# Memory attention on one core: softplus of the decay rates moved behind the gradient's squares, key scores and first layer in one product per batch, SiLU by ScalarE

## What is computed

```python
k, v, q = (causal_conv4(h @ W.T) for W in (Wk, Wv, Wq))           # [B, S, 64]
alpha = mean(sigmoid(h @ aW.T + ab) * 0.1)
eta   = mean(sigmoid(h @ eW.T + eb) * 0.9 + 0.05)
theta = mean(softplus(h @ tW.T + tb) * 0.1)
for each chunk of 128 tokens:                                      # 8 chunks
    g = grad over W of |silu(k @ W1.T) @ W2.T - v|^2, at the chunk's first state, * 0.1
    g = g * min(1 / |g|, 1)
    for t in chunk: S = eta*S - theta*g[t];  W = (1 - alpha)*W + S; keep W[t]
    out[t] = silu(q[t] @ W1[t].T) @ W2[t].T
out = rmsnorm(out @ Wo.T) * norm_g * (h @ gW.T + gb)
```

## Time and profile before

| what | value |
| --- | --- |
| median of 3 runs | 854.41 us (850.83 to 855.55) |
| profiled execution, its own time | 863.48 us |
| its span | 861.6 us |
| mean granted TensorE clock | 0.901 of full speed |
| TensorE busy | 721.4 us (84%) |
| VectorE busy | 605.4 us (70%) |
| ScalarE busy | 436.1 us (51%) |
| GpSimd busy | 249.9 us (29%) |

### The profile page before, as it was taken

One profiled execution on the slowest core, in us unless ns is written; L12 is line 12 of the kernel. 1 busy time (PEld: TensorE's weight loads), 2 busy tenths in 40 slices (PEclk: granted clock), 3 DMA queues, 4 the chain that ended last, 5 costly groups with the idle time before them and its releaser, 6 DMA issues. The chain is left out here.

```text
span 861.6 us, 15519 instructions
## 1 busy us (share of the span) xinstructions
PE 721.4 (84%) x5689; PEld 632.9 (73%) x5689; DVE 605.4 (70%) x1311; ACT 436.1 (51%) x1034; POOL 249.9 (29%) x185
## 2 busy tenths in 40 slices
PE   4449799995767999999999999999878238899996
PEld 2238799994566878888788887878756127799996
DVE  1877577843485978798888987977763655787761
ACT  1525457540636565665866568565432504475550
POOL 0053511314221143250623506142232045413202
PEclk9769899997888989999898999999977659999999
DMA  9975624613101012040130303103030723616300
GB/s 335 409 276 168 251 63 164 194 24 129 49 0 50 2 49 99 2 147 2 51 99 22 125 2 99 51 1 99 1 97 2 244 78 111 207 52 226 115 13 31
DMA packets 57858, 89.19 MB, mean 104 GB/s; under 512 B 6592, under 2 KB 48704, under 8 KB 57664
## 3 DMA queue, kind: packets, MB, share of 16 engines
q1 hardware_dynamic: 45808, 70.18, 23.5%
q0 software_dynamic: 3840, 10.49, 3.6%
q10 hardware_dynamic: 8144, 7.61, 3.0%
HBM read 74.63 MB, written 22.02 MB: 112 GB/s over the span
## 5 line engine op out<-in xcount | busy, mean ns | idle before, releaser
L626 PE MATMUL ps<-moe_normedT_high,weights_high_up 128*128 128x320 f32 x256 | 85.3, 333 | 11.4 <-DVE moe_hidden_low L484 7.2
L484 DVE SCALAR_TENSOR_TENSOR moe_hidden_low<-ps,moe_hidden_high 128x256 fp32r<-128x256 f32 x128 | 54.0, 422 | 40.7 <-ACT moe_hidden_high L589 36.5
L628 PE MATMUL ps<-moe_normedT_high,weights_low_up 128*128 128x320 f32 x256 | 82.4, 322 | 0.0
L627 PE MATMUL ps<-moe_normedT_low,weights_high_up 128*128 128x320 f32 x256 | 82.4, 322 | 0.0
L626 PE MATMUL ps<-weights_high_down,moe_hidden_high 128*128 128x256 f32 x256 | 73.4, 287 | 0.8 <-issue 0.8
L1079 POOL TENSOR_TENSOR att_o_rs<-att_o_mean,minus_half 128x4 f32<-128x4 f32 x16 | 16.2, 1013 | 197.3 <-DVE att_o_mean L1323 197.3
L628 PE MATMUL ps<-weights_high_down,moe_hidden_low 128*128 128x256 f32 x256 | 71.5, 279 | 0.8 <-issue 0.8
L627 PE MATMUL ps<-weights_low_down,moe_hidden_high 128*128 128x256 f32 x256 | 71.4, 279 | 0.0
L626 PEld LDWEIGHTS ps<-moe_normedT_high,weights_high_up 128*128 128x128 f32 x256 | 51.2, 200 | 14.2 <-DVE moe_hidden_low L484 6.1
L567 ACT CAST weights_high_down<-weights_raw_down 128x256 fp32r<-128x256 f32 x96 | 35.0, 408 | 42.2 <-PE ps L628 27.7
L588 ACT ACTIVATE moe_shared<-ps 128x64 f32<-128x64 f32 x128 | 29.0, 227 | 51.3 <-PE ps L628 44.7
(11 more groups left out here) (292 smaller groups left out, 2159.0 us busy)
## 6 DMA issues: line engine op xcount, KB each, us to landing
weights_raw_up<-in_w SPq DMA_DIRECT2D x16, 1024.0 KB
weights_raw_down<-in_w SPq DMA_DIRECT2D x16, 1024.0 KB
first_xt<-in_xT SPq DMA_DIRECT2D x8, 1024.0 KB, 7.9
weights_rows<-x SPq DMA_DIRECT2D x8, 1024.0 KB, 5.6
out_x<-weights_rows SPq DMA_DIRECT2D x8, 1024.0 KB, 4.4
weights_rows<-x ACTq DMA_DIRECT2D x7, 1024.0 KB, 5.5
weights_rows<-x SPq DMA_DIRECT2D x2, 512.0 KB, 4.4
weights_raw_up<-in_w_x SPq DMA_DIRECT2D x1, 704.0 KB
```

Of the source, the lines that this page charges most:

```text
L484: v.scalar_tensor_tensor(hidden_low[i][:, f, :], ps[:, 2 + (KF * i + f) % 3, WHOLE[i]], 0.0, hidden_high[i][:, f, :].bitcast(F32), ALU.max ...
L626: mm(dst, high_l, high_r, start=start, stop=False)
L627: mm(dst, high_l, low_r, start=False, stop=False)
L628: return mm(dst, low_l, high_r, start=False, stop=stop)
```

## The change

- Key scores and the first layer become one product per batch: the queries and W1 lie side by side in a tile QW (128 + 64 columns), and `queries_hidden` multiplies each batch's keys by 192 columns. Its first four batches go to pair A, the last four to pair C.
- SiLU is one ScalarE function (Silu) and, for its slope, a Tanh of half the argument: slope = 0.5 * (1 + hid - (hid - 1) * tanh). The sigmoids of alpha and eta are Tanh as well, with the scales folded into the rates. VectorE's two multiplications by the sigmoid are gone.
- `thetas` (Abs, Exp, Ln) of chunk c moves from the end of ScalarE's step c-1 to step c, between the squares of the gradient and the copy of the key/value projection; a Silu on one column follows it. Chunk 0's stays in the prologue.
- `turn_x` fills BB first and then A, and waits for the key squares and for P1; VectorE's key norms come after the first half of the gated output.
- The state is kept once less (2 x 64 columns instead of 3 x 64).

```diff
@@ VectorE
-            def scores(c):
-                dve.wait_ge(qk_made, c + 1)
-                v.tensor_tensor(P1[:], wide(A), M[:], ALU.mult).then_inc(p1_ready, 1)
-
-            def hidden(c, first):
-                dve.wait_ge(sig_ready, c + 1)
-                if not first:
-                    dve.wait_ge(hid_m_ready, c)
-                v.tensor_tensor(hid[:], wide(C)[:, :, 0:D], sig_h[:], ALU.mult).then_inc(hid_ready, 1)
+            def scores(c):
+                for h, src in enumerate((A, C)):
+                    dve.wait_ge(bend_ready if h else half_bent, c + h)
+                    last = v.tensor_tensor(in_fours(P1, h), key_products(src)[:, :, :, 0:CH], in_fours(M, h), ALU.mult)
+                last.then_inc(p1_ready, 1)
...
-            def second_hidden(c, par):
-                dve.wait_ge(sig2_ready, c + 1)
-                v.tensor_tensor(hid2[:], wide(DD), sig_h2[:], ALU.mult).then_inc(hid2_ready, 1)
...
                 if not last:
                     scores(c + 1)
+                gated_output(c, par, 0)
+                if not last:
                     key_norms(c + 1, 1 - par)
-                    hidden(c + 1, False)
-                gated_output(c, par, 0)
@@ ScalarE, last line of thetas
+                s.activation(unread[:], t["minus_half"][:, 0:1], ACT.Silu)
...
-            def hidden(c, first):
-                act.wait_ge(pre_made, c + 1)
-                if not first:
+            def hidden(c, h):
+                act.wait_ge(qk_made, 2 * c + h + 1)
+                if h == 0:
                     act.wait_ge(slope_ready, c)
-                s.activation(sig_h[:], wide(C)[:, :, 0:D], ACT.Sigmoid).then_inc(sig_ready, 1)
+                    act.wait_ge(hid_m_ready, c)
+                src = key_products(C if h else A)[:, :, :, CH:]
+                last = s.activation(in_fours(hid, h), src, ACT.Silu)
+                if h:
+                    last.then_inc(hid_ready, 1)
+                s.activation(in_fours(bend, h), src, ACT.Tanh, scale=0.5).then_inc(bend_ready if h else half_bent, 1)
...
-                s.activation(sig_h2[:], wide(DD), ACT.Sigmoid).then_inc(sig2_ready, 1)
+                s.activation(hid2[:], wide(DD), ACT.Silu).then_inc(hid2_ready, 1)
...
                 gradients(c)
+                if not first:
+                    thetas(c, par, False)
                 if not last:
                     kv_projection(c + 1)
...
                 if not last:
-                    thetas(c + 1, 1 - par, False)
+                    hidden(c + 1, 0)
                     keys(c + 1, False, final)
-                    hidden(c + 1, False)
+                    hidden(c + 1, 1)
@@ TensorE
-                for h, dst in enumerate((A, BB)):
+                for h, dst in enumerate((A, BB) if first else (BB, A)):
                     pe.wait_ge(x_normed, B * c + HALF * (h + 1))
                     if not first:
-                        pe.wait_ge(p1_ready if h == 0 else knorm_ready, c)
+                        pe.wait_ge(p1_ready if h else k_squared, c)
...
+            def queries_hidden(c, par):
+                pe.wait_ge(q_conv, TAPS * c + TAPS)
+                pe.wait_ge(state_copied, 2 * c)
+                pe.wait_ge(gate_read, 4 * c + 4)
+                for h, dst in enumerate((A, C)):
+                    if h:
+                        pe.wait_ge(gram_copied, c + 1)
+                        pe.wait_ge(lg_read, c)
+                    for j in range(HALF):
+                        b = h * HALF + j
+                        last = mm(key_products(dst)[:, j // 2, j % 2, :], KV[par][0:D, b, :], QW[0:D, b, :],
+                                  start=True, stop=True)
+                    last.then_inc(qk_made, 1)
...
                 keys(c + 1, 1 - par)
-                queries(c + 1, 1 - par)
-                hidden(c + 1, 1 - par, False)
+                queries_hidden(c + 1, 1 - par)
```

More of the change, by code:

```diff
@@ L860, in __init__ @@
         self.x2T = x2T.rearrange("p (k n) -> p k n", k=KH)
-        self.state = start[:, 0:3 * D * B].rearrange("p (b n) -> p b n", b=B)
+        self.state = start[:, 0:2 * D * B].rearrange("p (b n) -> p b n", b=B)
         self.norm_g = start[:, 3 * D * B:3 * D * B + H]
@@ L940, in memory_attention @@
     THETA, KNORM = two("THETA", [P, B]), two("KNORM", [P, B])
-    state, read_w = [given.state, sb("state1", [P, B, 3 * D])], given.read_w
-    sig_h, hid, slope = sb("sig_h", [P, B, D]), sb("hid", [P, B, D]), sb("slope", [P, B, D])
+    state, read_w = [given.state, sb("state1", [P, B, 2 * D])], given.read_w
+    bend, hid, slope = sb("bend", [P, B, D]), sb("hid", [P, B, D]), sb("slope", [P, B, D])
     hid_m = sb("hid_m", [P, B, 2, D])
@@ L1419, in turned @@
                     act.wait_ge(gate_made, 4 * c)
-                for h, src in enumerate((A, BB)):
+                for h, src in enumerate((A, BB) if first else (BB, A)):
                     act.wait_ge(x_turned, 2 * c + h + 1)
@@ L1471, in sigmoids @@
                     act.wait_ge(ends_ready, c)
-                s.activation(sig_ae, (BB if first else A).rearrange("p a n -> p (a n)"), ACT.Sigmoid,
-                             bias=b_ae[:, 0:1]).then_inc(ae_sig, 1)
+                s.activation(sig_ae, (BB if first else A).rearrange("p a n -> p (a n)"), ACT.Tanh,
+                             bias=half_b_ae[:, 0:1], scale=0.5).then_inc(ae_sig, 1)
             def rates(c, first):
@@ L1534, in new_state @@
                 new = wide(C)
-                s.copy(state[1 - par][:, :, 0:D], new[:, :, 0:D])
-                s.copy(state[1 - par][:, :, D:3 * D], new).then_inc(state_copied, 1)
+                s.copy(QW[0:D, :, CH:], new[0:D, :, 0:D])
+                s.copy(state[1 - par][:], new).then_inc(state_copied, 1)
                 s.copy(read_w[0:D, :, 0:D], new[0:D, :, D:P]).then_inc(state_copied, 1)
@@ L1613, in _ @@
             thetas(0, 0, True)
-            hidden(0, True)
+            first_hidden()
             step(0, 0, True, False)
@@ L1727, in hidden, with hidden_turned @@
                 last.then_inc(pre_made, 1)
-            def hidden_turned(c):
+            def hidden_turned(c, first=False):
                 pe.wait_ge(consts, 16 * len(loads))
                 pe.wait_ge(hid_ready, c + 1)
+                pe.wait_ge(bend_ready, c + 1)
+                if not first:
+                    pe.wait_ge(p1_ready, c + 1)
                 for b in range(B):
@@ L1750, in second_hidden @@
                     for rows in (slice(0, D), slice(D, P)):
-                        mm(wide(DD)[rows, b, :], state[par][:, b, rows], QAB[:, b, :], start=True, stop=False)
+                        mm(wide(DD)[rows, b, :], state[par][:, b, 0:D], QAB[:, b, :], start=True, stop=False)
                     for rows in (slice(0, D), slice(D, P)):
@@ L1766, in retrieve @@
                     for rows, b in pair_of(s):
-                        mm(paired[rows, s, :], state[par][:, b, 2 * D:3 * D], hid2_ab[:, b, :], start=True, stop=False)
+                        mm(paired[rows, s, :], state[par][:, b, D:2 * D], hid2_ab[:, b, :], start=True, stop=False)
                     for rows, b in pair_of(s):
@@ L1918, in _ @@
             queries(0, 0)
-            hidden(0, 0, True)
+            hidden(0)
             step(0, 0, True, False)
```

73 lines of the change are left out of this document (43 added, 30 removed).

## The result

The change makes the kernel slightly slower: 860.34 us median of 9 runs (854.72 to 865.14) against 854.41 (850.83 to 857.70, 9 runs), ratio 1.0063 with a 95% interval of 1.0032 to 1.0094. By the ratio that is +5.4 us, between +2.7 and +8.0. Slower was forecast, but with +12.5 us more than twice as much; 860.3 lies inside the stated range of 852 to 877.

What follows compares the result with a forecast made beforehand. TensorE's order was taken to bound the steps. Tails -24.5 and +2.2, heads +24.6 and -2.4, clock +12 and +2, last tail -1.4 gave +12.5 us: 867 us, own range 860 to 876, with rival 1 852 to 877.

Steps and rivals of the forecast that it cites:

- the stall: Head: TensorE's second turn waits 3.3 us for the result's first-half copy, starting 13.7 us after the hidden layer's turning (U).
- The block: Moved softplus plus one-column Silu on ScalarE, between gradient squares and key/value copy: 5.9 us, with three table loads.
- The clock: TensorE drops to half clock behind each head's wait: 2.0 us per head, bounds 0 and 3.4, +12 in all.
- The six heads: From the hidden layer's turning to the new state, chunks 1 to 6: +24.6, less 2.4, plus 12 for the clock.
- Rival 1: Same stall in the heads, but the clock holds: -1.5 us, 853 us, no change; chance 0.18.
- The tails: Seven step ends, new state to the hidden layer's turning: -24.5, +2.2 and +2 for loop jumps, -1.4 for the last.
- Two times: +2.2: Two tails where TensorE's loop jumps back: the old stall, no longer hidden, starts the hidden layer's turning 1.1 us later.
- I take it low, +1 each: Two tails with the loop's jump: TensorE's clock assumed low, +1 us each, +2 in all.
- 3.5 us less per tail: Each of seven tails, at full clock: the hidden layer's turning ends at 469.0 instead of 472.55, -24.5 us in all.
- that is not what decides the tail: Tail: merged products save TensorE 1.0 to 1.9 us, but this saving was said not to decide the tail.
- 3 (Silu and Tanh with different tables): Silu and Tanh need different tables, three more loads per tail: +27 us, 894 us or more; chance 0.05.
- 2: Exp and Ln share a table, one load fewer: block 4.6 us, stall 2.0, worth 7.7 us; 845 if clock holds; chance 0.13.

Runs made afterwards that it cites:

- experiment 3: Changed kernel with one table for Exp and Ln, it and the Silu/Tanh table loaded in ScalarE waits, none in the softplus block; ratio 0.9719 to before.
- experiment 4: Changed kernel with Exp and Ln replaced by Square, so no softplus and no loads in its block; ratio 0.9714 to before.
- experiment 2: The filler: changed kernel with 22 unread TensorE products in the wait for the copy of the result's first half, steps 1 to 6; ratio 0.9966 to before.
- experiment 5: Changed kernel with Exp and Ln from one table loaded at the block's head, two loads in the block instead of three; ratio 0.9908 to before.
- experiment 6: Changed kernel with key scores and first layer as two products per batch (128 and 64 columns) again; ratio 1.0126 to before.
- experiment 7: Changed kernel with the two products per batch apart and the eight batches' gram products as one, using batch 0's weights; ratio 1.0174 to before.
- experiment 1: Changed kernel with the next chunk's softplus put back at the end of ScalarE's step, before the new Silu and Tanh; ratio 1.0128 to before.
- experiment 8: Changed kernel with the softplus back at the step's end, its one Exp/Ln table loaded in ScalarE's wait for the outputs' first half; ratio 0.9907 to before.
- experiment 9: Kernel before with Exp and Ln replaced by Square, so no softplus and no table switches; ratio 0.9784 to before.
- experiment 10: Kernel before, computing everything, with one Exp/Ln table loaded in ScalarE's wait for the outputs' first half; ratio 0.9830 to before.

## Why the prediction was right in kind and wrong in size

**What bounds the kernel, and the stall: right.** The block came out at 5.93 us (5.9 forecast), the squares' end at U + 5.9 (U + 5.8), the second turn at U + 13.7 (U + 13.7), its wait at 3.0 us (3.3). Experiments 3 and 4 show the cause: with the loads out of the block the wait is gone. Three loads in a row behind the squares, the wait for L1581 in six steps, half clock behind it: all as listed under what the changed profile would show.

**The clock: right in this trace, a little dear.** I took 2.0 us per head. The filler gives 1.8, the two kinds of heads of experiment 5 give 1.6. The six heads together were forecast at +34.2 us (24.6 - 2.4 + 12) and measured at +32.2. Rival 1, the clock that holds, did not occur in the profiled execution of the changed kernel. It did behind the same wait of 3 us in six of the twelve heads of experiments 6 and 7, and at 1.9 us in four heads of six. That all six heads of the changed kernel paid for the clock is thus no property of the wait's length, and the other eight executions, which have no trace, may have paid less or more.

**The tails: this step failed, by size.** Forecast -21.7 us (-24.5, +2.2, +2, -1.4), measured -28.4. Two terms were mis-sized:
- *"Two times: +2.2" and "I take it low, +1 each".* I carried the stall of the earlier trace rows into the new tail, 4.2 us in all. It does not occur there: all five tails of steps 1 to 5 take 34.0 us, and the branch back takes 0.2 us instead of 3.3 and 3.5. Experiment 6 shows that each stall would have cost 3.9 us (38.8 against 34.9), more than I thought; two of them would have added 7.8 us, by estimate, and brought the sum near the forecast. It isn't the merging that removes it, since the slow branch is there with merged products in experiments 1, 2 and 8. Why it is gone in the changed kernel stays open.
- *"3.5 us less per tail".* Measured are 3.9 (37.9 to 34.0 in most plain tails), some 0.4 more. ScalarE's second Tanh was over at 462.72, 3.56 us after the products began, against 3.8 in my schedule. The products took 2.86 us, not 2.6, and "that is not what decides the tail" was wrong as well: in experiment 6 the 0.9 us that TensorE needs more appears in every plain tail.

The two tails with the jump gained 8.4 us where the forecast has 2.8; the other five make up the rest of the 6.7 us between forecast and measured tails. The remainder is the heads' 2.0, in the same direction.

**Why that spoiled the sum.** The forecast was the difference of two terms of 34 and 22 us; the true ones are 32.2 and 28.4. They are off by 6% and by 24%, and the difference of +12.5 becomes +3.8, with 5.4 (2.7 to 8.0) measured. That the range held the time is partly luck. It had no bound for a tail that gains more: its own part, 860 to 876, varied the clock and slow plain tails only, and 860.3 lies at its edge for another reason than the cheap clock that this edge stands for. Only rival 1 took it down to 852.

**The rivals.** 3 (Silu and Tanh with different tables) is refuted: 23 loads in the attention part instead of 24, none between Silu and Tanh. 2 did not occur in the changed kernel, but its mechanism is real when it is asked for: with one table for Exp and Ln the wait is 1.1 us shorter (experiment 5). The Trainium skill counts 2.66 us for a switch ("ScalarE: Activation LUTs", What ACT_TABLE_LOAD costs). The traces disagree, also in the new order: from the start of a load to that of the next activation in the block it is 1.29 to 1.30 us. The set with both Exp and Ln that the Trainium skill names (same page, Table sets) serves both functions in experiment 3.

## What to carry to other kernels

A table load waits for no data: in experiment 3 two loads a step lay in waits of ScalarE and cost nothing. So it belongs into one of that engine's waits, with a table that serves all functions of the block; moving the block with its loads from one critical chain to another only moves the cost. Before moving work on an in-order engine, count what is queued behind it at the new place against the slack there: here 5.9 us met 1.6. A stall of TensorE can have a second price behind it, half clock over dense work, which came in some heads and not in others of the same code. And where a forecast is the difference of two large terms, its range should come from theirs.

## What the runs showed of the hardware

- An idle TensorE of 1.9 us was followed by 3.4 us at half clock in two heads and by full clock in four, with the same instructions (experiment 5); one of 3 us was followed by it in all six heads of the changed kernel and in three of six in experiments 6 and 7 each. With 2.7 us of products that nobody reads in the wait (experiment 2) it did not occur in any of the six.
- Where TensorE's loop of two steps jumps back, the branch takes 3.3 to 4.3 us in some kernels (before, experiments 2, 6, 7, 8, 9, 10, and one jump of two in experiment 1) and 0.2 us in others (changed, experiments 3, 4, 5, and the other jump of experiment 1). TensorE starts nothing for 1.6 to 2.6 us at a slow branch, or for 1.2 to 1.3 in experiment 2, unless it waits for ScalarE there anyway (experiments 1 and 8).
- The slow branches go together with packets on the queue that fetches instructions. From 395 to 605 us, where both jumps of each kernel lie, that queue brings 17 or 18 packets in the kernels with two slow branches, 10 in experiment 1, and 0 or 1 in those with none; in the kernel before, packets start at 413.3 and 516.7 us, within the branches of 412.25 and 515.66. That one causes the other was not tried. The number of TensorE's instructions does not decide it, as the changed kernel and experiments 1 and 8 have the same. What does was not found.
- 16 matmuls of 64 rows took 1.99 us with 64 columns, 2.05 with 128 and 2.86 with 192, by the durations of their rows: from 64 to 128 columns they became hardly longer.
